# Two attention layers on one core: keys and values as three one-pass fp32r products of split operands

## The chip, the cores and the metric

The kernel runs on one core of a Trainium2 chip. Its engines are TensorE (PE), VectorE (DVE), ScalarE (ACT), GpSimd (POOL) and SyncE (SP, which only issues DMA here). The metric is the device time of one execution in microseconds.

## What is computed

Two layers follow each other. The first (`L0`) mixes x (16 x 64 x 256) with itself, guided by a context `ctx_2048` of the same shape; the second (`L1`) is a transformer block whose keys and values come from the context:

```python
x_q = einsum('oc,bcn->bno', w_qk, y);  x_k = einsum('oc,bcn->bon', w_qk, x)
x_v = einsum('oc,bcn->bon', w_v, x) + b_v
attention = softmax(x_q @ x_k);  attention /= 1e-07 + attention.sum(axis=1)
x_r = x_v @ attention
x   = x + relu(w_t @ (x - x_r) + b_t)                      # layer 0

q = layer_norm(x, ln1) @ q_w + q_b                         # layer 1, 16 heads of 16
k = encoder @ k_w + k_b
v = encoder @ v_w + v_b
hidden = softmax(q k^T / 4, masked) @ v @ cproj_w + cproj_b + x
out = hidden + gelu(layer_norm(hidden, ln2) @ fc_w + fc_b) @ proj_w + proj_b
```

All inputs are fp32 (the mask is boolean). The change touches only how `k` and `v` are formed from the encoder states, which are the context.

## The kernel before, in words

The 16 batches are taken as N = 8 pairs of 128 rows. Every engine walks the same list of steps `t` (`for t in STEPS`, -1 to 20), written out by hand; what an engine does in a step stands in its block in a fixed order, and an instruction that waits holds up all that follow it on that engine.

Steps 0 to 8 hold layer 0. In step t PE makes the energies of pair t (`gx,ys`), the projections of pair t+1 (`rows,gram` and `wtvT,rows`) and the mix of pair t-1 (`att,us`); DVE makes the row maxima (`nmax`, L683), copies the projections out of PSUM (`gx` L688, `uext` L696), takes reciprocals (`rinv` L604) and normalises (`mixn`, `rin`); ACT makes the exponentials (`att`, L443); POOL scales (`us`, L344), adds the residual (L325) and finds the inverse deviation (`rstd`, L308) that DVE's `xn` (L641, x1_norm) waits for; POOL's bias addition (L333) waits in turn for `xn`. From step 9 on (AT = 9) layer 1's attention runs, and from step 15.6 on the MLP.

Keys and values are made in between, in twelve units (`UNITS`, L207) that all pass through one PSUM bank, FILL. For each half of the tokens (h = 0, 1; 512 tokens) there are two "ctx" units, which turn two pairs of context rows each (`ident,ys`, L826) and which ACT copies to `ctxT` (L417); two "keys" units of two 512-column fp32 products each (L833); and two "values" units of four 256-column products each (L840). The next unit waits until ACT has emptied the bank (`free_fill`, L809). The tables at L208 to L211 place them: ctx units of the first half in steps -1 and 0, keys in 0 and 1, values in 1 and 2; ctx units of the second half in steps 4 and 6, keys in 7 and 8, values in 9 and 11. `wk` and `wv` are the fp32 weights of keys and values.

The MLP's weights and inputs are already split: a high part rounded to fp32r and the remainder as a low part (`high_part` on DVE, L636; `low_part` on POOL, L320), multiplied as high-high, high-low and low-high. `SPLIT` (L215) puts one weight part into each of the steps 1 to 7; the buffers `ff[0]`, `ff[1]` are used only once the MLP runs.

Of the kernel before, what the change touches and what calls it, by code (L numbers as in the profile page):

```python
# [13 lines left out]
P = 128  # L14
# [13 lines left out]
def xattn_two_layers(nc, A, out):  # L28
# [24 lines left out]
    with ExitStack() as ctx:  # L53
# [3 lines left out]
        def sem(name):  # L57
# [18 lines left out]
        keys_b = sb("keys_b", [P, G, 2])  # L76
        half_power = sb("half_power", [P, 1])
        wq = sb("wq", [P, G, D])
        wk = sb("wk", [P, G, D])
        wv = sb("wv", [P, G, D])  # L80
        wc = sb("wc", [P, G, D])

        wstage = sb("wstage", [P, 2, W])
# [9 lines left out]

        rows = sb("rows", [P, N, D])
        ys = sb("ys", [P, N, D])
        ctxT = sb("ctxT", [P, G, TOK])
        keys = sb("keys", [P, G, 2, N * P])
        vals = sb("vals", [P, N, 2, HP, 2 * HD])
        gx = sb("gx", [P, 2, D])
# [28 lines left out]
        act_ff = ys[:, 0:4, :].rearrange("p (k a) d -> p k (a d)", k=2)  # L128
        ff = [sb("ff_hi", [P, M, TOK], F32R), sb("ff_lo", [P, M, TOK], F32R)]

        psum = ctx.enter_context(nc.psum_tensor("psum", [P, 8, BANK], F32))

        PROJ0, ENERGY, MIX, WTX, TURN, FILL = 0, 1, 3, 5, 6, 7
# [18 lines left out]
            "mask_ready", "mask_zeroed", "is_row_ready", "select_ready", "parity_ready", "keys_b_ready",  # L152
                                                                   "stored"))
        S = {k: sem(k) for k in (
            "part_hi part_lo ctx_turned ctx_ready keys_made keys_ready values_made values_ready "
            "proj_made proj_ready energy_made energy_max energy_exp rowsum_inv scaled_u mixed wtx_made colsum_ln "
            "colsum_inv mix_normed relu_in relu_out x1_ready x1_stats x1_meanvar x1_vareps x1_rstd x1_normed x1_turned "
            "x1t_ready queries_made queries_ready x1_plus_bias scores_made scores_max scores_shifted "
# [9 lines left out]
        def bank(n):  # L168
            return psum[:, n, :]
# [41 lines left out]
        FILL_C = {N: 9, AT: 10}  # L211

        UNITS_BEFORE = [9, 11]
        WARM_UP = 6
        SPLIT = {1: 0, 2: 1, 3: 2, 4: 3, 5: 4, 6: 5, 7: 6, AT + 5: 7}  # L215

# [67 lines left out]
        def _(pool):  # L284
# [42 lines left out]
            def x1_plus_bias(n):  # L327
# [4 lines left out]
                wait(pool, "x1_normed", n + 1)  # L332
                pool.tensor_tensor(rows[:, n, :], rows[:, n, :], cproj_b[:], ALU.add).then_inc(S["x1_plus_bias"], 1)  # L333

            for t in STEPS:

                n = t
                if 0 <= n < N:

# [7 lines left out]
                if 0 <= t - 2 < N - 1:  # L347
                    residual(t - 2)
                if t == 0:
                    for name, w, s in (("cproj_b", cproj_b, "cb"), ("proj_b", proj_b, "pb")):  # L350
                        src = A["L1_xattn_" + name].rearrange("(o d) -> o d", o=1).broadcast_to([P, D])
                        pool.dma_start(w[:], src).then_inc(w_loaded[s], 16)
# [50 lines left out]
        def _(act):  # L403
# [7 lines left out]
            def fill(unit):  # L411
                kind, h, i = unit
                if kind == "ctx":
                    wait(act, "ctx_turned", 2 * h + i + 1)

                    wait(act, "values_made", 2 * h)
                    act.copy(ctxT[:, :, 2 * i * P:2 * (i + 1) * P].rearrange("p g (a t) -> p a g t", a=2),  # L417
                             bank(FILL).rearrange("p (a g t) -> p a g t", a=2, g=G)).then_inc(S["ctx_ready"], 1)
                if kind == "keys":
                    wait(act, "keys_made", 2 * h + i + 1)  # L420
                    if h == i == 0:
                        act.wait_ge(keys_b_ready, G)
                    for a in range(2):
                        identity(keys[:, i, a, h * TOK:(h + 1) * TOK], bank(FILL), keys_b[:, i, a:a + 1],
                                 parity[:, a:a + 1], "keys_ready")
                if kind == "values":
                    wait(act, "values_made", 2 * h + i + 1)
                    if h == i == 0:
                        act.wait_ge(zeros_ready, 3)
                    n = NH * h + 2 * i  # L430
                    for e in range(2):
                        src = psum[e * C:(e + 1) * C, FILL, :].rearrange("p (a i b d) -> p a i b d", a=2, b=2, d=HD)
                        for b in range(2):
                            act.copy(vals[b * C:(b + 1) * C, n:n + 2, e, :, b * HD:(b + 1) * HD],
                                     src[:, :, :, b, :]).then_inc(S["values_ready"], 1)
# [126 lines left out]
        def _(dve):  # L562
# [64 lines left out]
            def inverse_of_sum(n, i):  # L627
# [2 lines left out]
                dve.reciprocal(pinv[:, n % 2, HEAD_HALVES[i]],  # L630
                               psums[:, n % 2, HEAD_HALVES[i]]).then_inc(S["probs_inv"], 1)

            def high_part(c):
                dve.wait_ge(part_loaded[c % 2], 16 * (c // 2 + 1))
                src, hi, lo = part(c)
                dve.tensor_copy(hi, src).then_inc(S["part_hi"], 1)  # L636
# [38 lines left out]

            for t in STEPS:

                n = t
                if 0 <= n < N:
                    for e in range(2):  # L680
# [5 lines left out]
                if 0 <= n < N:  # L686
                    wait(dve, "proj_made", n + 1)
                    dve.tensor_copy(gx[:, n % 2, :], halfbank(PROJ0, 0)).then_inc(S["proj_ready"], 1)  # L688
                    wait(dve, "scaled_u", 4 * (n - 1))
                    if n == 0:  # L690
                        dve.wait_ge(wtbv_made, 1)
                        dve.tensor_copy(wtbv[:], psum[:, SETUP_WTBV, 0:P]).then_inc(wtbv_ready, 1)
                        dve.wait_ge(wtbv_ready, 1)
                        dve.wait_ge(zeros_ready, 3)
                    dst = uext[:, n % 2, :, :].rearrange("p j (b c) -> p j b c", b=3)[:, :, 0:3:2, :]
                    dve.tensor_tensor(dst, halfbank(PROJ0, 1).rearrange("p (j b c) -> p j b c", j=2, b=2),  # L696
                                      wtbv[:].rearrange("p (b c) -> p b c", b=2).unsqueeze(1)
                                      .broadcast_to([P, 2, 2, C]), ALU.add).then_inc(S["proj_ready"], 1)
                if 0 <= t - 4 < N - 3:
                    x1_norm(t - 4)  # L700
                if 0 <= t < N:
# [9 lines left out]
                if t == 0:  # L711
# [5 lines left out]
                    for g in range(G):  # L717
                        dve.tensor_scalar(keys_b[:, g, :], parity[:], col(K_B + g), None,
                                          ALU.mult).then_inc(keys_b_ready, 1)
                if 0 <= t < N and t in SPLIT:  # L720
                    high_part(SPLIT[t])
                if t == 5:
# [59 lines left out]
        def _(pe):  # L782
# [26 lines left out]
            def free_fill(i):  # L809

                if i > 0:
                    kind, h, k = UNITS[i - 1]
                    wait(pe, *{"ctx": ("ctx_ready", 2 * h + k + 1), "keys": ("keys_ready", 2 * (2 * h + k + 1)),
                               "values": ("values_ready", 4 * (2 * h + k + 1))}[kind])

            def fill(i):
# [10 lines left out]
                                               ys[:, n, g * P:(g + 1) * P], ident[:])  # L827
                    ins.then_inc(S["ctx_turned"], 1)
                if kind == "keys":
                    pe.wait_ge(w_loaded["k"], 16)  # L830
                    wait(pe, "ctx_ready", 2 * (h + 1))
                    for c in range(G):
                        ins = mm(bank(FILL), wk[:, c, k * P:(k + 1) * P], ctxT[:, c, :], c == 0, c == G - 1)  # L833
                    ins.then_inc(S["keys_made"], 1)
                if kind == "values":
                    pe.wait_ge(w_loaded["v"], 16)
                    for a in range(2):
                        tok = slice((2 * k + a) * P, (2 * k + a + 1) * P)
                        for c in range(G):
                            ins = mm(halfbank(FILL, a), ctxT[:, c, tok], wv[:, c, :], c == 0, c == G - 1)  # L840
                    ins.then_inc(S["values_made"], 1)

            def mlp_unit(h, unit):
# [217 lines left out]
```

## Time and profile before

| | us |
|---|---|
| median of three runs | 170.68 |
| lowest, highest | 170.66, 171.85 |
| the profiled execution | 171.03 |
| its span in the trace | 169.2 |

Busy, of the span: PE 146.0 us (86%), DVE 101.1 (60%), ACT 98.6 (58%), POOL 87.0 (51%). The chain of work that ended last lies on PE for 57%, on POOL for 17% and on DVE for 9%. "Idle before" in a row is the time that the engine waited, with the instruction that released it. An fp32 matmul is recorded as two matmuls, so "x4" in the trace are two products of the program; an fp32r matmul is recorded once. Recorded durations of PE overlap, so costs are read from one start to the next.

### The profile page before, as it was taken

The numbers are of one execution on the slowest core, as the hardware profiler recorded it, in microseconds if no ns is written. First come the engines' busy times: TensorE is split into PE (matmuls) and PEld (weight loads), VectorE is DVE, ScalarE is ACT, GpSimd is POOL, SyncE is SP. The second block draws the span as 40 slices with busy tenths as digits, with TensorE's granted clock in tenths as the row PEclk, the third lists the DMA queues.
The fourth block names the chain that finished last, engine by engine and source line by source line (L and its number), as shares of the span: only waits on it lengthen the run. The fifth ranks groups of instructions, "written<-read, shape, count | busy, mean of one in ns | idle before, by whom it ended". The sixth has DMA issues, their size and how long they took to land.

```text
span 169.2 us, 3520 instructions
## 1 busy us (share of the span) xinstructions
PE 146.0 (86%) x1260; PEld 111.3 (66%) x1260; DVE 101.1 (60%) x243; ACT 98.6 (58%) x242; POOL 87.0 (51%) x146
## 2 busy tenths in 40 slices
PE   7599999999986888197998665957999999999993
PEld 6365678788754264074675544645787999888993
DVE  2435525897975343990589797795678521488221
ACT  2017977789769755735778667966967333344000
POOL 8935617468888952572431976799361634000000
PEclk9969999999999999759999999999999999999999
DMA  1995320202101200000000000000000010000001
GB/s 50 344 326 175 66 62 0 66 0 62 43 25 62 62 0 0 0 6 0 0 4 6 0 4 0 4 0 0 4 0 0 4 61 32 31 0 6 31 31 62
DMA packets 6786, 6.89 MB, mean 41 GB/s; under 512 B 1044, under 2 KB 6194, under 8 KB 6770
## 3 DMA queue, kind: packets, MB, share of 16 engines
q1 hardware_dynamic: 5808, 5.85, 11.1%
q10 hardware_dynamic: 674, 0.56, 1.0%
q0 software_dynamic: 288, 0.27, 0.9%
q8 instruction: 10, 0.16, 0.4%
q14 instruction: 6, 0.05, 0.1%
HBM read 5.62 MB, written 1.05 MB: 39 GB/s over the span
## 4 chain that ended last, share of the span: by engine, by line
PE 57%; POOL 17%; DVE 9%; issue 7%; DMA 4%; ACT 3%; ACTq 1%; POOLq 0%
PE psum L784 53%; DMA ys<-in_ctx_dram 4%; POOL probs L381 4%; POOL us L344 3%; POOL rstd L308 2%; PE psum L1019 2%; POOL wfc_lo L320 2%; POOL wpj_lo L320 1%; DVE smax L738 1%; POOL hidT_lo L372 1%; POOL rows L325 1%; POOL rows L389 1%; DVE psums L625 1%; DVE probs L749 1%; DVE xn L641 1%
## 5 line engine op out<-in xcount | busy, mean ns | idle before, releaser
L381 POOL TENSOR_TENSOR probs<-probs,pinv 128x512 f32<-128x512 f32 x16 | 16.5, 1055 | 9.7 <-DVE pinv L630 9.7
L344 POOL TENSOR_SCALAR us<-uext,rinv 128x128 f32<-128x128 f32 x32 | 12.4, 399 | 13.9 <-DVE rinv L604 13.3
L784 PE MATMUL psum<-wpj_hi,ff_hi 128*128 128x256 f32 x64 | 18.3, 287 | 0.0
L784 PE MATMUL psum<-wpj_hi,ff_lo 128*128 128x256 f32 x64 | 18.1, 283 | 0.0
L784 PE MATMUL psum<-wpj_lo,ff_hi 128*128 128x256 f32 x64 | 18.1, 283 | 0.0
L398 ACT ACTIVATE ys<-psum,vec 128x512 f32<-128x512 f32 x16 | 10.9, 687 | 9.3 <-PE psum L784 9.2
L683 DVE TENSOR_REDUCE nmax<-psum 128x2 f32<-128x512 f32 x16 | 10.3, 685 | 9.9 <-PE psum L784 9.9
L784 PE MATMUL psum<-att,us 128*128 128x256 f32 x64 | 15.2, 381 | 0.7 <-POOL us L344 0.7
L625 DVE TENSOR_REDUCE psums<-probs 128x8 f32<-128x512 f32 x16 | 10.6, 660 | 8.5 <-ACT probs L540 8.3
L443 ACT ACTIVATE att<-psum,nmax 128x256 f32<-128x256 f32 x32 | 14.7, 471 | 0.3 <-DVE nmax L683 0.2
L784 PE MATMUL psum<-hidT_hi,wfc_hi 128*128 128x512 f32 x32 | 13.2, 414 | 1.1 <-POOL hidT_lo L372 1.1
L784 PEld LDWEIGHTS psum<-att,us 128*128 128x128 f32 x64 | 11.9, 190 | 3.1 <-POOL us L344 1.2
L670 DVE TENSOR_TENSOR rows<-psum,rows 128x256 f32<-128x256 f32 x8 | 3.4, 426 | 16.9 <-PE psum L784 16.9
L661 DVE CAST ff_hi<-ys 128x512 fp32r<-128x512 f32 x16 | 7.3, 457 | 8.9 <-ACT ys L398 8.7
L784 PE MATMUL psum<-hidT_hi,wfc_lo 128*128 128x512 f32 x32 | 12.6, 394 | 0.0
L784 PE MATMUL psum<-hidT_lo,wfc_hi 128*128 128x512 f32 x32 | 12.6, 394 | 0.0
L784 PEld LDWEIGHTS psum<-wpj_hi,ff_hi 128*128 128x128 f32 x64 | 12.1, 189 | 0.1
L784 PEld LDWEIGHTS psum<-wpj_lo,ff_hi 128*128 128x128 f32 x64 | 12.1, 188 | 0.1
L784 PEld LDWEIGHTS psum<-wpj_hi,ff_lo 128*128 128x128 f32 x64 | 12.1, 189 | 0.0
L372 POOL TENSOR_TENSOR hidT_lo<-hidf,hidT_hi 128x256 fp32r<-128x256 f32 x8 | 6.2, 778 | 11.0 <-ACT hidT_hi L534 11.0
L663 DVE TENSOR_TENSOR ff_lo<-ys,ff_hi 128x512 fp32r<-128x512 f32 x16 | 11.1, 692 | 0.5
L540 ACT ACTIVATE probs<-probs 128x512 f32<-128x512 f32 x16 | 9.4, 623 | 2.6 <-DVE probs L749 2.6
(115 smaller groups left out, 367.6 us busy)
## 6 DMA issues: line engine op xcount, KB each, us to landing
wstage<-in_L_xattn_fc_w_dram SPq DMA_DIRECT2D x4, 256.0 KB, 5.2
wstage<-in_L_xattn_proj_w_dram SPq DMA_DIRECT2D x4, 256.0 KB, 2.7
out_dram<-rows SPq DMA_DIRECT2D x8, 128.0 KB, 1.7
ys<-in_ctx_dram SPq DMA_DIRECT2D x1, 512.0 KB, 6.3
rows<-in_x_dram SPq DMA_DIRECT2D x1, 512.0 KB, 7.4
ys<-in_ctx_dram ACTq DMA_DIRECT2D x1, 384.0 KB, 7.0
rows<-in_x_dram SPq DMA_DIRECT2D x1, 384.0 KB, 5.8
wk<-in_L_xattn_k_w_dram SPq DMA_DIRECT2D x1, 256.0 KB, 6.7
```

The lines of the kernel that those rows point to most:

```text
L320: pool.tensor_tensor(lo, src, hi.bitcast(F32), ALU.subtract).then_inc(S["part_lo"], 1)
L344: pool.tensor_scalar(us[:, n % 2, e, j, :], uext[:, n % 2, j, e * C:e * C + P], rinv[:, n % 2, e, j:j + 1], 1.0, ALU.mult, ALU.mult).then_ ...
L372: pool.tensor_tensor(hidT[1][:, :, cols], hidf[:], hidT[0][:, :, cols].bitcast(F32), ALU.subtract).then_inc(S["hid_lo"], 1)
L381: pool.tensor_tensor(half, half, pinv[:, n % 2, k].unsqueeze(2).broadcast_to([P, H // 2, C]), ALU.mult).then_inc(S["probs_ready"], 1)
L398: act.activation(act_ff[:, k % 2, :], bank(k % 4), ACT.Gelu_apprx_tanh, bias=col(FC_B + unit[1])).then_inc(S["gelu_ready"], 1)
L443: act.activation(att[:, n % 2, e, j, :], halfbank(ENERGY + e, j), ACT.Exp, bias=nmax[:, n % 2, e, j:j + 1], accum_out=rsum[:, n % 2, e, j: ...
L540: act.activation(half, half, ACT.Exp, scale=SCALE).then_inc(S["probs_exp"], 1)
L625: dve.tensor_reduce(psums[:, n % 2, HEAD_HALVES[i]], half, AX.X, ALU.add).then_inc(S["probs_sum"], 1)
L661: dve.tensor_copy(ff[0][:, m, :], act_ff[:, k % 2, :]).then_inc(S["ff_hi"], 1)
L663: dve.tensor_tensor(ff[1][:, m, :], act_ff[:, k % 2, :], ff[0][:, m, :].bitcast(F32), ALU.subtract).then_inc(S["ff_lo"], 1)
L683: dve.tensor_reduce(nmax[:, n % 2, e, :], bank(ENERGY + e).rearrange("p (j m) -> p j m", j=2), AX.X, ALU.max, negate=True).then_inc(S["ene ...
L784: return pe.matmul(dst, lhsT, rhs, start=start, stop=stop)
```

## The change

Context, `wk` and `wv` are split in a part rounded to fp32r and a remainder. Both parts live in the buffers `ff[0]` (high) and `ff[1]` (low), which are free until the MLP: context in columns 0 and 1, the key weight in 2, the value weight in 3. Therefore they are called ff_hi and ff_lo in the rows of the changed kernel.

- ACT's copy of the turned context now writes the rounded part. DVE makes the remainder, out of the PSUM bank (`ctx_low`), twice in step 0 and once each in steps 4 and 6. PE's next use of the bank, and the keys units, wait for the remainder.
- DVE rounds each weight (`weight_high`), POOL subtracts (`weight_low`), both in step 0.
- A keys unit is six fp32r products of 512 columns instead of two in fp32; a values unit twelve of 256 instead of four.

```diff
+            def weight_low(w, s):
+                wait(pool, f"w{s}_hi", 1)
+                hi, lo = wkr if s == "k" else wvr
+                pool.tensor_tensor(lo, w[:], hi.bitcast(F32), ALU.subtract).then_inc(S[f"w{s}_lo"], 1)
...
+            def ctx_low(h, i):
+                wait(dve, "ctx_ready", 2 * h + i + 1)
+                cols = slice(2 * i * P, 2 * (i + 1) * P)
+                dve.tensor_tensor(ctxT[1][:, :, cols].rearrange("p g (a t) -> p a g t", a=2),
+                                  bank(FILL).rearrange("p (a g t) -> p a g t", a=2, g=G),
+                                  ctxT[0][:, :, cols].bitcast(F32).rearrange("p g (a t) -> p a g t", a=2),
+                                  ALU.subtract).then_inc(S["ctx_lo"], 1)
+
+            def weight_high(w, s):
+                dve.wait_ge(w_loaded[s], 16)
+                dve.tensor_copy((wkr if s == "k" else wvr)[0], w[:]).then_inc(S[f"w{s}_hi"], 1)
...
-                    wait(pe, *{"ctx": ("ctx_ready", 2 * h + k + 1), "keys": ("keys_ready", 2 * (2 * h + k + 1)),
+                    wait(pe, *{"ctx": ("ctx_lo", 2 * h + k + 1), "keys": ("keys_ready", 2 * (2 * h + k + 1)),
...
                 if kind == "keys":
-                    pe.wait_ge(w_loaded["k"], 16)
-                    wait(pe, "ctx_ready", 2 * (h + 1))
+                    wait(pe, "wk_lo", 1)
+                    wait(pe, "ctx_lo", 2 * (h + 1))
                     for c in range(G):
-                        ins = mm(bank(FILL), wk[:, c, k * P:(k + 1) * P], ctxT[:, c, :], c == 0, c == G - 1)
+                        for a, b in ((0, 0), (0, 1), (1, 0)):
+                            ins = mm(bank(FILL), wkr[a][:, c, k * P:(k + 1) * P], ctxT[b][:, c, :],
+                                     c == 0 and a + b == 0, c == G - 1 and a == 1)
                     ins.then_inc(S["keys_made"], 1)
                 if kind == "values":
-                    pe.wait_ge(w_loaded["v"], 16)
+                    wait(pe, "wv_lo", 1)
```

On DVE, steps -1 and 0 read as follows before; the row of maxima (`nmax`) opens step 0, and a name in brackets is what an instruction waits for:

```order
L696 TENSOR_TENSOR uext<-psum,wtbv 128x2x2x64 [waits zeros_ready,wtbv_ready]
L683 TENSOR_REDUCE nmax<-psum 128x2 [waits energy_made] x2
L688 COPY gx<-psum 128x256 [waits proj_made]
L696 TENSOR_TENSOR uext<-psum,wtbv 128x2x2x64
L604 RECIPROCAL rinv<-rsum 128x2 [waits energy_exp] x2
L714 COPY vec<-psum 128x22 [waits vec_turned]
```

and now (`ff_lo<-psum,ff_hi` is the context's remainder, `ff_hi<-wk` and `ff_hi<-wv` the rounded weights):

```order
L723 TENSOR_TENSOR uext<-psum,wtbv 128x2x2x64 [waits zeros_ready,wtbv_ready]
L648 TENSOR_TENSOR ff_lo<-psum,ff_hi 128x2x2x128 [waits ctx_ready]
L655 CAST ff_hi<-wk 128x512 [waits w_loaded_k]
L710 TENSOR_REDUCE nmax<-psum 128x2 [waits energy_made] x2
L715 COPY gx<-psum 128x256 [waits proj_made]
L723 TENSOR_TENSOR uext<-psum,wtbv 128x2x2x64
L648 TENSOR_TENSOR ff_lo<-psum,ff_hi 128x2x2x128 [waits ctx_ready]
L655 CAST ff_hi<-wv 128x512 [waits w_loaded_v]
L616 RECIPROCAL rinv<-rsum 128x2 [waits energy_exp] x2
L744 COPY vec<-psum 128x22 [waits vec_turned]
```

One remainder and one cast stand ahead of the maxima, one of each between `uext` and the reciprocals that POOL waits for.

At the end of step 4 and the start of step 5, DVE before:

```order
L595 BN_AGGR mv<-stats 128x2 [waits x1_stats]
L636 CAST wfc_hi<-wstage 128x512 [waits part_loaded1]
L683 TENSOR_REDUCE nmax<-psum 128x2 [waits energy_exp,energy_made] x2
L688 COPY gx<-psum 128x256 [waits proj_made]
L696 TENSOR_TENSOR uext<-psum,wtbv 128x2x2x64 [waits scaled_u]
L641 TENSOR_SCALAR xn<-rows,mv,rstd 128x256 [waits x1_rstd]
```

and now:

```order
L607 BN_AGGR mv<-stats 128x2 [waits x1_stats]
L648 TENSOR_TENSOR ff_lo<-psum,ff_hi 128x2x2x128 [waits ctx_ready]
L660 CAST wfc_hi<-wstage 128x512 [waits part_loaded1]
L710 TENSOR_REDUCE nmax<-psum 128x2 [waits energy_exp,energy_made] x2
L715 COPY gx<-psum 128x256 [waits proj_made]
L723 TENSOR_TENSOR uext<-psum,wtbv 128x2x2x64 [waits scaled_u]
L665 TENSOR_SCALAR xn<-rows,mv,rstd 128x256 [waits x1_rstd]
```

The remainder, which waits for ACT's copy of the turned context, came in ahead of the cast, the maxima and `xn`. In step 6 it stands in the same way between `mv` and the cast, ahead of the maxima of step 7.

On PE the values unit of step 9 had four products, and has now twelve, of which the last six stand here (`ff_hi` alone is high times high):

```order
L816 MATMUL psum<-ff_hi 128x256
L816 MATMUL psum<-ff_lo,ff_hi 128x256
L816 MATMUL psum<-ff_hi,ff_lo 128x256
L816 MATMUL psum<-ff_hi 128x256
L816 MATMUL psum<-ff_lo,ff_hi 128x256
L816 MATMUL psum<-ff_hi,ff_lo 128x256
L916 MATMUL psum<-ident,xn 128x128 x2
```

against, before:

```order
L784 MATMUL psum<-wv,ctxT 128x256 x4
L880 MATMUL psum<-ident,xn 128x128 x2
```

Each fp32 product has become three; the turn of x1 (`ident,xn`) still stands behind the unit.

## Rows read from the trace of the kernel before

**Rows 1.** Busy time by stretch: stretch, then busy us (count) of PE, PEld, DVE, ACT, POOL; clock, DMA.

```profile
30.00:40.00 10.00, 10.00 (x60) 7.92 (x58) 9.23 (x26) 7.92 (x27) 6.18 (x13) 1.00 0.09 28
...
50.00:60.00 10.00, 7.22 (x23) 3.56 (x22) 5.17 (x17) 8.81 (x24) 8.45 (x17) 1.00 0.18 52
```

**Rows 2.** PE in order of time, MLP: start, duration, operation, [idle before].

```profile
116.46 0.40 PE L784 MATMUL psum<-hidT_lo,wfc_hi 128*128 128x512 f32 x1
...
118.79 0.40 PE L784 MATMUL psum<-hidT_hi,wfc_lo 128*128 128x512 f32 x1
...
132.20 0.28 PE L784 MATMUL psum<-wpj_hi,ff_lo 128*128 128x256 f32 x1
...
133.63 0.28 PE L784 MATMUL psum<-wpj_hi,ff_lo 128*128 128x256 f32 x1
```

**Rows 3.** PE in order of time, steps 0 to 2: keys, values and the mixes behind them.

```profile
13.68 1.98 PE L784 MATMUL psum<-ctxT,wk 128*128 128x512 f32 x4
...
17.64 1.94 PE L784 MATMUL psum<-ctxT,wk 128*128 128x512 f32 x4
19.42 1.89 PE L784 MATMUL psum<-att,us 128*128 128x256 f32 x8
...
25.53 1.89 PE L784 MATMUL psum<-wv,ctxT 128*128 128x256 f32 x8
27.26 1.89 PE L784 MATMUL psum<-att,us 128*128 128x256 f32 x8
```

**Rows 4.** All engines in order of time, steps 0 and 1: DVE and ACT.

```profile
12.14 1.29 DVE L683 TENSOR_REDUCE nmax<-psum 128x2 f32<-128x512 f32 x2 [2.37 <-PE psum L784]
...
12.74 0.59 ACT L417 COPY ctxT<-psum 128x512 f32<-128x512 f32 x1 [1.75 <-PE psum L826]
...
13.96 0.41 DVE L696 TENSOR_TENSOR uext<-psum,wtbv 128x256 f32<-128x256 f32 x1
...
19.62 1.45 ACT L409 ACTIVATE keys<-psum,keys_b,parity 128x512 f32<-128x512 f32 x2 [0.21 <-PE psum L784]
```

**Rows 5.** Groups by line and shape, DVE and POOL: busy us, mean ns of one.

```profile
L749 DVE TENSOR_TENSOR probs<-psum,smax 128x512 f32<-128x512 f32 x16 | 10.3, 684 | 0.2
...
L636 DVE CAST wfc_hi<-wstage 128x512 fp32r<-128x512 f32 x4 | 1.7, 417 | 0.0
...
L320 POOL TENSOR_TENSOR wfc_lo<-wstage,wfc_hi 128x512 fp32r<-128x512 f32 x4 | 5.1, 1272 | 0.0
```

**Rows 6.** All engines in order of time, end of step 4 and step 5.

```profile
39.46 0.58 ACT L417 COPY ctxT<-psum 128x512 f32<-128x512 f32 x1
39.51 1.29 DVE L683 TENSOR_REDUCE nmax<-psum 128x2 f32<-128x512 f32 x2 [0.27 <-PE psum L784]
...
42.17 0.41 DVE L641 TENSOR_SCALAR xn<-rows,mv,rstd 128x256 f32<-128x256 f32 x1 [0.71 <-POOL rstd L308]
...
42.67 0.73 POOL L333 TENSOR_TENSOR rows<-rows,cproj_b 128x256 f32<-128x256 f32 x1 [0.53 <-DVE xn L641]
```

**Rows 7.** All engines in order of time, steps 6 and 7.

```profile
51.18 0.58 ACT L417 COPY ctxT<-psum 128x512 f32<-128x512 f32 x1
...
52.92 0.46 ACT L443 ACTIVATE att<-psum,nmax 128x256 f32<-128x256 f32 x1
...
57.09 1.96 PE L784 MATMUL psum<-x1T,wq 128*128 128x512 f32 x4 [0.62 <-issue]
```

**Rows 8.** All engines in order of time, the seam of the two layers.

```profile
71.98 0.40 PE L784 MATMUL psum<-maskrow,select 32*128 32x256 bf16 x4 [3.69 <-DVE probs L749]
...
73.89 3.22 PE L784 MATMUL psum<-wv,ctxT 128*128 128x256 f32 x8
...
78.22 1.98 PE L784 MATMUL psum<-x1T,wq 128*128 128x512 f32 x4 [0.90 <-ACT x1T L409]
...
88.93 1.23 DVE L738 TENSOR_REDUCE smax<-psum 128x16 f32<-128x1024 f32 x1 [0.52 <-PE psum L784]
```

**Rows 9.** Busy time by stretch, PE alone: stretch, PE busy us (count), granted clock, DMA.

```profile
74.00:75.00 1.00, 1.00 (x4) 0.50 0.00 0
```

More of the change, by code:

```diff
@@ L78, in xattn_two_layers @@
         wq = sb("wq", [P, G, D])
-        wk = sb("wk", [P, G, D])
-        wv = sb("wv", [P, G, D])
         wc = sb("wc", [P, G, D])
@@ L95, in xattn_two_layers @@
         ys = sb("ys", [P, N, D])
-        ctxT = sb("ctxT", [P, G, TOK])
         keys = sb("keys", [P, G, 2, N * P])
@@ L129, in xattn_two_layers @@
         ff = [sb("ff_hi", [P, M, TOK], F32R), sb("ff_lo", [P, M, TOK], F32R)]
+        ctxT = [ff[0][:, 0:G, :], ff[1][:, 0:G, :]]
+        wkr = [ff[k][:, 2:3, :].rearrange("p o (g n) -> p (o g) n", g=G) for k in range(2)]
+        wvr = [ff[k][:, 3:4, :].rearrange("p o (g n) -> p (o g) n", g=G) for k in range(2)]
+        wk = sb("wk", [P, G, D])
+        wv = sb("wv", [P, G, D])
         psum = ctx.enter_context(nc.psum_tensor("psum", [P, 8, BANK], F32))
@@ L154, in xattn_two_layers @@
         S = {k: sem(k) for k in (
-            "part_hi part_lo ctx_turned ctx_ready keys_made keys_ready values_made values_ready "
+            "part_hi part_lo wk_hi wk_lo wv_hi wv_lo ctx_turned ctx_ready ctx_lo keys_made keys_ready values_made values_ready "
             "proj_made proj_ready energy_made energy_max energy_exp rowsum_inv scaled_u mixed wtx_made colsum_ln "
@@ L213, in xattn_two_layers @@
         UNITS_BEFORE = [9, 11]
+        CTX_LOW = (4, 6)
         WARM_UP = 6
@@ L333, in x1_plus_bias @@
                 pool.tensor_tensor(rows[:, n, :], rows[:, n, :], cproj_b[:], ALU.add).then_inc(S["x1_plus_bias"], 1)
+            def weight_low(w, s):
+                wait(pool, f"w{s}_hi", 1)
+                hi, lo = wkr if s == "k" else wvr
+                pool.tensor_tensor(lo, w[:], hi.bitcast(F32), ALU.subtract).then_inc(S[f"w{s}_lo"], 1)
             for t in STEPS:
+                if t == 0:
+                    weight_low(wk, "k")
                 n = t
@@ L349, in _ @@
                 if t == 0:
+                    weight_low(wv, "v")
                     for name, w, s in (("cproj_b", cproj_b, "cb"), ("proj_b", proj_b, "pb")):
@@ L416, in fill @@
                     wait(act, "values_made", 2 * h)
-                    act.copy(ctxT[:, :, 2 * i * P:2 * (i + 1) * P].rearrange("p g (a t) -> p a g t", a=2),
+                    act.copy(ctxT[0][:, :, 2 * i * P:2 * (i + 1) * P].rearrange("p g (a t) -> p a g t", a=2),
                              bank(FILL).rearrange("p (a g t) -> p a g t", a=2, g=G)).then_inc(S["ctx_ready"], 1)
@@ L676, in _ @@
             for t in STEPS:
+                if t == 0:
+                    ctx_low(0, 0)
+                    weight_high(wk, "k")
                 n = t
@@ L698, in _ @@
                                       .broadcast_to([P, 2, 2, C]), ALU.add).then_inc(S["proj_ready"], 1)
+                if t == 0:
+                    ctx_low(0, 1)
+                    weight_high(wv, "v")
                 if 0 <= t - 4 < N - 3:
@@ L719, in _ @@
                                           ALU.mult).then_inc(keys_b_ready, 1)
+                if t in CTX_LOW:
+                    ctx_low(1, CTX_LOW.index(t))
                 if 0 <= t < N and t in SPLIT:
@@ L839, in fill @@
                         for c in range(G):
-                            ins = mm(halfbank(FILL, a), ctxT[:, c, tok], wv[:, c, :], c == 0, c == G - 1)
+                            for x, y in ((0, 0), (0, 1), (1, 0)):
+                                ins = mm(halfbank(FILL, a), ctxT[x][:, c, tok], wvr[y][:, c, :],
+                                         c == 0 and x + y == 0, c == G - 1 and x == 1)
                     ins.then_inc(S["values_made"], 1)
```

## The prediction

> **What bounds the kernel now.** I read the busy time by stretch first, then the instructions in order of time. Over 30 to 40 us DVE is busy 9.23 of 10 us and PE's records cover all 10 [rows 1]: two engines are full in the stretch where the change adds work to one and takes it from the other. So a sum of PE time saved says nothing yet; each place has to be asked which wait ends last there. There are four: step 0 of the first layer (12 to 30 us), the turn of context rows in steps 4 and 6 (38 to 57 us), and the seam between the layers with its values units (72 to 89 us). From 116 us on, the MLP has no changed instruction.
>
> **What one unit saves on PE.** A values unit is four fp32 products of 256 columns, eight records, 25.53 to 27.26: 1.73 us, 0.216 a record [rows 3]. A keys unit is two fp32 products of 512 columns, four records of twice that, 1.73 us again; from 17.64 to the next work at 19.42 the trace has 1.78 [rows 3], so 0.05 is a gap that stays. What the new units cost is shown by the MLP, which already multiplies split fp32r operands three ways: at 512 columns 10 starts lie in 118.79 - 116.46 = 2.33 us, 0.233 each; at 256 columns 12 starts in 133.63 - 132.20 = 1.43 us, 0.119 each [rows 2]. Six of the first are 1.40 us, twelve of the second 1.43 us. A keys unit saves 0.33 us, a values unit 0.30 us; all eight save 2.5 us. At 256 columns, three fp32r passes cost nearly as much as the fp32 they replace, so the prize is small from the start.
>
> The Trainium skill ("TensorE: Matmul & The Clock Gate", section "Back-to-back issue gap") gives N / 2.4 + 2.5 ns for a matmul on its own at the full clock, 216 and 109 ns at these sizes. By it the units would take 1.30 and 1.31 us, and my total would be about 0.5 us lower; the rows of this kernel's own fp32r products are 0.233 and 0.119, and I go by them.
>
> **Step 0: PE waits for DVE.** Before, the first keys unit starts at 13.68, soon after ACT's second copy of the turned context, which ends at 12.74 + 0.59 [rows 3, 4]. Now it needs both low parts and the weight's low part. The price of a low part on DVE is taken from the nearest row, a subtraction out of PSUM at 128x512: 0.684 us; a cast of that size to fp32r takes 0.417 on DVE, a subtraction to fp32r 1.272 on POOL [rows 5]. The first low part and the first weight cast, 1.1 us together, fall into DVE's idle 2.37 us before 12.14 [rows 4] and cost nothing; were that cover gone, 1.1 us. The weight's low part then runs on POOL to about 13.5, before anyone asks for it. The second low part is queued behind two maxima, gx and uext: 13.96 + 0.41 + 0.68 = 15.05, so the keys unit starts at 15.1, **1.4 us late**, and ends 1.4 - 0.33 = 1.07 late. The next energies and their exponentials on ACT are that late. The second keys unit gives back 0.33, but the values unit behind it waits for its bank, which ACT empties from 19.62 on, after step 1's exponentials [rows 4]: that copy is 1.07 late too. Less two values units, 0.60, this leaves +0.47 at the mix at 27.26. Behind the second low part on DVE stand also a second weight cast and the reciprocals that POOL's scaling waits for; those come 1.2 us later, but the mix that needs them (19.42) is itself later. I take **+0.5**. Bounds: 0 if the low part costs only a cast's 0.42 and the rest sinks into the small idles at 39.5 and 42 us [rows 6], and 1.1 if ACT and DVE keep the whole delay.
>
> **Step 4: DVE waits for ACT.** (Times here and for step 6 are those of before, without the start's +0.5.) The low part is put ahead of DVE's weight cast and of the maxima of step 5 (39.51). It waits for ACT's copy, 39.46 + 0.58 = 40.04 [rows 6]. So: low part 40.07 to 40.75, cast to 41.17, maxima from 41.2, **1.7 us late**. What stands behind them on DVE is gx, uext and then xn, which before waited 0.71 us for POOL's rstd and started at 42.17 [rows 6]; 0.71 of the delay goes into that wait: xn starts at 41.2 + (42.17 - 0.71 - 39.51) = 43.15, 0.98 late. POOL waits for this xn (idle 0.53 before its bias addition at 42.67), and then does its low part of the MLP weight and the next scaling, without a pause. This ring POOL, DVE, POOL sets the pace of steps 4 to 7, so **+1.0** is passed on. Bounds 0.7 (low part at 0.42) and 1.6 (at 1.27, POOL's price for the same operation).
>
> **Step 6: the same again.** ACT's copy ends at 51.18 + 0.58 = 51.76; low part and cast bring the maxima of step 7 to 52.9; the first of the two (half of 1.29) is ready at 53.55. ACT's exponentials, which before began at 52.92 behind ACT's own chain, start at 53.6: **+0.65** on top [rows 7]. From them hang DVE's reciprocal and relu input, ACT's x1T and so the queries product at 57.09, which waits (0.62 idle) [rows 7]. On POOL's ring alone it would be 0.4; the exponentials decide. Bounds 0.4 and 1.2. The keys unit in between (0.33 saved) lies in PE's idle time and gives nothing; nor does the one in step 8, behind which PE idles 3.69 us for DVE before 71.98 [rows 8]. The loads of the MLP weights wait for POOL's low parts and move with them.
>
> **The seam.** The values unit at 73.89 runs at a granted clock of 0.50, the 1.2 GHz level [rows 9], and its eight records take 3.22 us; right behind it come the turn of x1 and ACT's x1T, for which PE waited 0.90 before 78.22 [rows 8]. No row shows fp32r at that level. Sixteen column passes become twelve; between the full-clock 0.30 and a quarter of 3.22, 0.8, I take **-0.45**, since the clock comes back before its end. The last values unit, in step 11, is followed by scores for which DVE waited 0.52 before 88.93 [rows 8]: all of **-0.30** is passed on.
>
> **Sum.** +0.5 + 1.0 + 0.65 - 0.45 - 0.30 = +1.4 us. The profiled execution took 171.03 (span 169.2), 0.35 over the median of 170.68; on the median the forecast is 172.1 us, 0.8% slower.
>
> **Rivals.**
> - *Not slower: the ring has more room than it shows.* If POOL's ring and not DVE sets every step from 4 on, DVE's late maxima cost only what exceeds its waits. Against it: that wait was 0.71 us at 42.17 where 1.7 is asked. From 1.7 us of slack on it would decide; then both middle terms fall and 0.5 - 0.75 remains, 170.4 us. Chance 0.18.
> - *The clock.* PE now idles 1.4 us before the first keys unit. If the granted clock fell there, each unit until it rose would take about 3.2 us for 1.7, as at 73.89 [rows 8, 9]; a keys and a values unit or what stands between them, +2.4 on the rest: 174.5 us. For it: 3.69 us of idleness stand ahead of the half clock there. Against it: 1.4 us is shorter, and between 50 and 60 us PE was idle for 2.8 of 10 us, 0.62 of it before 57.09, at a clock of 1.00 [rows 1, 7]. The skill's same page (section "Part 1: The HAM clock gate") also has idleness lower the clock. Chance 0.05.
> - *Nothing is absorbed.* Steps 4 and 6 cost 1.7 and 2.1 in full, because the exponentials and not xn carry on each time: 0.5 + 3.8 - 0.75 = 3.5, 174.2 us. Chance 0.07.
> - *As summed:* 0.70, by itself 171.2 to 173.0.
>
> **The numbers.** Range 170.3 to 173.4. 1% of the median is 1.7 us, about what a measurement of this kernel tells from no change, so the line to "slower" is at 172.4. A third of my own case lies above it (0.23), and the clock and the full delays (0.12): 0.35. Faster by 1% would need 169.0; even all 2.5 us saved with no delay gives 168.2, and the first rival's lower edge leaves 0.04. The rest, 0.61, is within 1%. It reaches from just below the first rival's 170.4 to 173.4, beyond my own case's upper end; the last two rivals and the first one's lower edge, under 0.2, lie outside.
>
> **What would show it.** After: keys unit from about 15.1 us with DVE named as releaser; low parts of 0.65 to 0.7 us on DVE; an idle time of about 1.1 us on DVE before the third and fourth, ended by ACT; maxima of step 5 near 41.7 and of step 7 near 54.4 (start delay included); x1T products at 59 rather than 57.1. It is wrong if fp32r products between fp32 ones take more than the MLP's spacing, if DVE meets ACT's copy already done, or if POOL's ring swallows the delay.

## The result

The changed kernel takes 172.62 us (median of 20 runs, 170.78 to 174.8) where the kernel before, run beside it on the same chip, takes 171.13 (169.91 to 173.29): ratio 1.0068, 95% interval 1.0034 to 1.0101. That is slower, by less than the 1% that a measurement here tells from no change. The forecast was 172.1 us and a ratio of 1.008. The medians go over all executions and differ by 1.5 us; the ratio, here and for every run below, compares only the executions outside a slower state, which 6 of the 20 of after were in, and stands for 1.2 us (0.6 to 1.7).

The profiled execution of after took 174.69 us, 2.1 more than its median, with a span of 172.9, against 171.03 and 169.2 before. So the difference in span, 3.7 us, must not be read as the change's price; it is taken apart below. The busy times of after, over the whole span:

```profile
PE 147.5 (85%) x1284; PEld 115.5 (67%) x1284; DVE 104.8 (61%) x249; ACT 98.7 (57%) x242; POOL 89.6 (52%) x148
```

**Step 0** (all engines, in order of time: start, duration, engine, line, operation, [idle before and what ended it]), the counterpart of [rows 3, 4]:

```profile
14.91 0.68 DVE L648 TENSOR_TENSOR ff_lo<-psum,ff_hi 128x512 fp32r<-128x512 f32 x1
...
15.74 0.47 PE L816 MATMUL psum<-ff_hi 128*128 128x512 f32 x1 [1.37 <-DVE ff_lo L648]
16.05 0.40 PE L816 MATMUL psum<-ff_lo,ff_hi 128*128 128x512 f32 x1
...
21.00 1.46 ACT L421 ACTIVATE keys<-psum,keys_b,parity 128x512 f32<-128x512 f32 x2
...
28.04 1.89 PE L816 MATMUL psum<-att,us 128*128 128x256 f32 x8
```

PE stands still for 1.37 us and the row names DVE's low part as what ended it. ACT's copy of the keys from the second keys unit (21.00) has no wait in brackets any more; before, it had one of 0.21 [rows 4].

**Steps 4 and 5**, the counterpart of [rows 6], same view:

```profile
40.23 0.58 ACT L429 CAST ff_hi<-psum 128x512 fp32r<-128x512 f32 x1
...
40.84 0.69 DVE L648 TENSOR_TENSOR ff_lo<-psum,ff_hi 128x512 fp32r<-128x512 f32 x1 [1.20 <-ACT ff_hi L429]
41.21 0.73 POOL L330 TENSOR_TENSOR rows<-rows,rout 128x256 f32<-128x256 f32 x1
41.45 0.77 DVE L660 CAST wfc_hi<-wstage 128x512 fp32r<-128x512 f32 x1
42.14 1.27 DVE L710 TENSOR_REDUCE nmax<-psum 128x2 f32<-128x512 f32 x2
...
44.00 0.40 DVE L665 TENSOR_SCALAR xn<-rows,mv,rstd 128x256 f32<-128x256 f32 x1
...
44.48 0.73 POOL L338 TENSOR_TENSOR rows<-rows,cproj_b 128x256 f32<-128x256 f32 x1 [1.57 <-DVE xn L665]
```

DVE, which was full here, now waits 1.20 us for ACT; `xn` no longer waits for POOL's `rstd`, and POOL waits 1.57 us for `xn` where it waited 0.53 [rows 6].

**Steps 6 and 7**, the counterpart of [rows 7]:

```profile
53.61 0.69 DVE L648 TENSOR_TENSOR ff_lo<-psum,ff_hi 128x512 fp32r<-128x512 f32 x1 [1.20 <-ACT ff_hi L429]
...
54.22 0.67 DVE L660 CAST wpj_hi<-wstage 128x512 fp32r<-128x512 f32 x1
...
54.81 1.28 DVE L710 TENSOR_REDUCE nmax<-psum 128x2 f32<-128x512 f32 x2
...
55.52 0.47 ACT L455 ACTIVATE att<-psum,nmax 128x256 f32<-128x256 f32 x1 [0.69 <-DVE nmax L710]
...
59.50 1.96 PE L816 MATMUL psum<-x1T,wq 128*128 128x512 f32 x4 [1.22 <-issue]
```

ACT's exponentials did not wait before [rows 7]; now the row names DVE's maxima, 0.69 us.

**The seam**, the counterpart of [rows 8]:

```profile
74.40 0.40 PE L816 MATMUL psum<-maskrow,select 32*128 32x256 bf16 x4 [3.68 <-DVE probs L781]
...
76.16 0.56 PE L816 MATMUL psum<-ff_hi 128*128 128x256 f32 x1
...
78.86 0.63 PE L916 MATMUL psum<-ident,xn 128*128 128x128 f32 x2
80.39 3.77 PE L816 MATMUL psum<-x1T,wq 128*128 128x512 f32 x4 [0.90 <-ACT x1T L421]
```

Busy time of after by stretch, PE alone (stretch, PE busy us (count), granted clock, DMA share, GB/s):

```profile
82.00:84.00 2.00, 2.00 (x4) 0.50 0.00 0
84.00:86.00 2.00, 2.00 (x12) 1.00 0.00 0
```

The queries product that took 1.98 us before [rows 8] takes 3.77 here: the clock is still 0.50 up to 84 us, where before it was 1.00 again by 78.

**Where 3.7 us went.** Marks found in every trace cut the span into stretches: DVE's first maxima (before at 12.14, [rows 4]), those of step 3 (30.24), the first row maximum `smax` of the second layer (68.27), its fourth (88.93, [rows 8]) and the start of the last result row (166.66). In after the first maxima start at 12.77, the last row at 170.31, and between them:

```profile
31.02 1.29 DVE L710 TENSOR_REDUCE nmax<-psum 128x2 f32<-128x512 f32 x2 [1.94 <-PE psum L816]
...
70.69 1.19 DVE L770 TENSOR_REDUCE smax<-psum 128x16 f32<-128x1024 f32 x1
...
92.58 1.23 DVE L770 TENSOR_REDUCE smax<-psum 128x16 f32<-128x1024 f32 x1 [0.21 <-PE psum L816]
```

The first maxima start 0.63 us later. The part in front of them differs from trace to trace by more (they start between 11.27 and 13.17 in the traces below), and the first low part did not delay them: they start 1.85 us behind the first energies of the step, before (10.29) as after (10.92). The stretches, in us:

| stretch | before | after | difference | forecast |
|---|---|---|---|---|
| 1: first maxima to those of step 3 | 18.10 | 18.25 | +0.15 | +0.5 |
| 2: to first `smax` of layer 2 | 38.03 | 39.67 | +1.64 | +1.65 |
| 3: to fourth `smax` | 20.66 | 21.89 | +1.23 | -0.75 |
| 4: to the last result row | 77.73 | 77.73 | 0.00 | 0 |

With the start's 0.63 these are the 3.65 us between the two last rows. Stretch 3 holds the clock's late return: 3.77 - 1.98 = 1.79 for the queries product alone. In two of the experiments that have the same fp32r products and an early return it is 20.01 and 19.82 (runs 1 and 2), -0.65 and -0.84 against before. With these the change's own part is 0.15 + 1.64 - 0.75 = about +1.0 us. But the same two traces are 0.35 and 0.50 us longer in stretch 4, where the clock falls once more (see runs 5 and 6), so that stretches 3 and 4 together give only -0.30 and -0.34; counted so, the change costs about +1.5. Whether this lengthening of stretch 4 belongs to the change is not shown. The measured 1.2 us (0.6 to 1.7) fits both.

### The profile page after: what moved, and what is told of

Its sections match the earlier page's. It is cut to its first block, busy times and chain, and to the rows that moved or that the text cites. A ratio compares the mean times of both kernels' runs of the same rounds, so it can differ in the third digit from the quotient of the medians.

```text
span 172.9 us, 3576 instructions
## 1 busy us (share of the span) xinstructions
PE 147.5 (85%) x1284; PEld 115.5 (67%) x1284; DVE 104.8 (61%) x249; ACT 98.7 (57%) x242; POOL 89.6 (52%) x148
## 3 DMA queue, kind: packets, MB, share of 16 engines
HBM read 5.62 MB, written 1.05 MB: 39 GB/s over the span
## 4 chain that ended last, share of the span: by engine, by line
PE 57%; POOL 14%; DVE 12%; issue 8%; ACT 4%; DMA 3%; POOLq 0%; DVEq 0%; ACTq 0%
PE psum L816 53%; POOL probs L393 4%; DMA vec_rows<-in_L_xattn_b_t_dram 3%; POOL us L355 2%; POOL rstd L313 2%; PE psum L1055 2%; POOL wfc_lo L325 1%; DVE smax L770 1%; POOL hidT_lo L384 1%; ACT x1T L421 1%; DVE mixn L622 1%; POOL rows L401 1%; DVE psums L637 1%; DVE nmax L710 1%; DVE probs L781 1%
## 5 line engine op out<-in xcount | busy, mean ns | idle before, releaser
L816 PE MATMUL psum<-x1T,wq 128*128 128x512 f32 x16 | 9.6, 728 | 2.8 <-issue 1.9
```

The lines of the kernel that those rows point to most:

```text
L816: return pe.matmul(dst, lhsT, rhs, start=start, stop=stop)
```

## The experiments

Each run was timed beside the kernel before (median 171.63 us for runs 1 to 4, 171.01 for 5 to 8). "After" is always the changed kernel; stretches are those of the table above, and a table at the end has them for all runs.

### 1. The remainders of steps 4 and 6 one place later

Theory: the two delays come from where the low part stands on DVE, ahead of the maxima, not from its 0.69 us of work. Rival: POOL's ring would have absorbed them anyway.

```
-                if t in CTX_LOW:
-                    ctx_low(1, CTX_LOW.index(t))
...
+                if t - 1 in CTX_LOW:
+                    ctx_low(1, CTX_LOW.index(t - 1))
                 if 0 <= t - 4 < N - 3:
                     x1_norm(t - 4)
```

> The changed kernel with one thing moved: the third and fourth context remainders on DVE stand in steps 5 and 7, behind gx and uext and ahead of xn, where DVE waited 0.71 and 1.74 us for POOL before the change. My theory: steps 4 and 6 cost 1.06 and 0.59 us in the trace of the changed kernel only because DVE stood waiting for ACT's copy with the maxima behind it. Then DVE's two idle times of 1.20 us ended by ACT are gone, xn of step 5 and 7 come when POOL's rstd lets them, and the time falls by 1.65 us, from a ratio of 1.007 to about 0.997 of the kernel before. Rival: the ring through POOL sets the pace and DVE's late maxima cost nothing. Then the ratio stays at 1.007.

Measured: 171.21 us, ratio 0.9989 (0.995 to 1.0028). Stretch 2 is 37.97 us, before 38.03, after 39.67: the whole +1.64 is gone. DVE of this run, in order of time:

```profile
38.23 0.45 DVE L660 CAST wfc_hi<-wstage 128x512 fp32r<-128x512 f32 x1
...
40.81 0.68 DVE L648 TENSOR_TENSOR ff_lo<-psum,ff_hi 128x512 fp32r<-128x512 f32 x1
41.59 0.41 DVE L665 TENSOR_SCALAR xn<-rows,mv,rstd 128x256 f32<-128x256 f32 x1
...
51.43 0.68 DVE L648 TENSOR_TENSOR ff_lo<-psum,ff_hi 128x512 fp32r<-128x512 f32 x1
...
53.23 0.41 DVE L665 TENSOR_SCALAR xn<-rows,mv,rstd 128x256 f32<-128x256 f32 x1 [1.12 <-POOL rstd L313]
```

The same two operations of 0.68 us now meet ACT's copy already done, and lie in the time in which `xn` waits for POOL's `rstd` anyway: at 53.23 it still waits 1.12 us behind the second. The work is the same; the place cost 1.64 us. This speaks against the ring's slack: with the remainders ahead of the maxima nothing of these 1.64 us was swallowed. Moving them had one more effect: the casts behind them, 0.77 and 0.67 us in after, are back at 0.45 and 0.39 here, so a part of the delay was theirs (last section). The whole time came 0.2% above the 0.997 expected, within its interval.

### 2. The second remainder of step 0 ahead of gx and uext

Theory: PE's wait in step 0 is DVE's order, and shrinks by the 0.8 us of `gx` and `uext`. The weight cast for the values moves behind `keys_b`.

```
+                if t == 0:
+                    ctx_low(0, 1)
                 n = t + 1
...
-                if t == 0:
-                    ctx_low(0, 1)
-                    weight_high(wv, "v")
...
+                    weight_high(wv, "v")
```

> The changed kernel with step 0 alone rearranged on DVE: the second context remainder right behind step 0's maxima, the value weight's cast at the end of the step. The first keys unit should start about 0.5 us later than before the change instead of 1.4. My theory, which put the start term at +0.5 (the trace of the changed kernel has only +0.15 by step 3): PE bounds steps 0 to 2, so the 0.9 us come through to step 3 and the ratio falls from 1.007 to about 1.002. Rival: the full DVE and ACT of steps 2 to 4 swallow them, and the ratio stays at 1.007.

Measured: 172.17 us, ratio 1.0055 (1.0017 to 1.0093). DVE and PE of this run in order of time:

```profile
14.62 0.69 DVE L648 TENSOR_TENSOR ff_lo<-psum,ff_hi 128x512 fp32r<-128x512 f32 x1 [0.17 <-ACT ff_hi L429]
...
15.46 0.47 PE L816 MATMUL psum<-ff_hi 128*128 128x512 f32 x1 [0.45 <-DVE ff_lo L648]
```

PE waits 0.45 us instead of 1.37, 0.92 less. Stretch 1 is 17.57 us, 0.68 below after and 0.53 below before; the other 0.24 went into a later turn of the context rows: ACT's copy of it starts 0.84 us behind the first maxima here (14.01), 0.59 in after (13.36). The whole time, expected at 1.002, does not separate this kernel from after (1.0068). Stretch 2 is 39.67, exactly after's: the two parts do not touch each other.

### 3. Both placements

The edits of 1 and 2 together.

> Both rearrangements at once. If the terms add up as I think: -1.65 and -0.9 against the changed kernel, a ratio of about 0.992, faster than the kernel before, since only the savings on PE are left. If either rival holds (POOL's ring, or DVE and ACT full in steps 2 to 4), 0.997 to 1.007.

Measured: 170.1 us, ratio 0.9934 (0.9897 to 0.997). Stretch 1 is 17.57, stretch 2 38.02: the sum of the two, with nothing lost. So the one-pass products do save time once the low parts stand where DVE or ACT is not asked for anything: 0.53 us in stretch 1, and 0.66% in all, which by itself is also under the 1% that a measurement tells from no change, though its interval leaves 1 out.

### 4. fp32 products on the new waits

After, but the keys and values units multiply the unrounded weights by the rounded context in fp32, two and four products as before; the remainders are made and waited for but not used, so the product with the context's remainder is left out of what is computed. The keys unit is shown; the values unit is changed in the same way.

```
-                        for a, b in ((0, 0), (0, 1), (1, 0)):
-                            ins = mm(bank(FILL), wkr[a][:, c, k * P:(k + 1) * P], ctxT[b][:, c, :],
-                                     c == 0 and a + b == 0, c == G - 1 and a == 1)
+                        ins = mm(bank(FILL), wk[:, c, k * P:(k + 1) * P], ctxT[0][:, c, :].bitcast(F32),
+                                 c == 0, c == G - 1)
```

> The changed kernel with all of its splitting and all of its waits, but with PE's keys and values units as two and four fp32 products again, of the fp32 weights with the rounded context; the remainders are made and not used. It measures what the cheaper products on PE give back. My theory: 0.33 and 0.30 us for each of the four units in steps 0 to 2 (1.3 in all, of which the ACT copy of keys may hide a part), 0.5 and 0.3 in the seam, nothing for the two keys units of steps 7 and 8: +1.8 us, a ratio of about 1.017. If PE's units were off the path, the ratio would stay at 1.007.

Measured: 175.1 us, ratio 1.0209 (1.0149 to 1.0268). PE in order of time:

```profile
15.97 1.95 PE L816 MATMUL psum<-ff_hi,wk 128*128 128x512 f32 x4 [1.37 <-DVE ff_lo L648]
...
29.46 1.89 PE L816 MATMUL psum<-att,us 128*128 128x256 f32 x8
```

The wait is again 1.37 us. Stretch 1 is 19.71: with the waits alone it is 19.71 - 18.10 = 1.61 us over before, and after is 19.71 - 18.25 = 1.46 below it. Neither is pure: the keys unit starts 15.97 - 12.74 = 3.23 us behind the first maxima here and 15.74 - 12.77 = 2.97 in after, at the same wait. This 0.26 is again the later turn of the context rows (ACT's copy at 13.59, 0.85 behind the maxima). Without it the delay costs 1.35 and the cheaper units give back 1.20, near the 1.26 that four of them save by the forecast's prices. Stretch 2 is 39.68, as in after: the cheaper keys units of steps 7 and 8 give nothing. The ratio is a little above the 1.017 expected.

### 5 and 6. The clock kept up across the seam

To see the seam without the half clock, eight products nobody reads are put into PE's 3.7 us of idleness, once into the kernel before and once into after:

```
                 if t == N:
                     turn_x1(N - 3)
+                    wait(pe, "relu_in", N)
+                    for _ in range(8):
+                        mm(halfbank(WTX, 0), ident[:], wq[:, 0, :])
```

> The kernel before with one addition: eight fp32 products of 256 columns on PE, into a free PSUM bank and read by nobody, in the stretch where PE idles 3.69 us for DVE between the two layers. They do no work of the kernel and should take 3.4 us of that idle time. Theory: the granted clock of 0.50 in the seam comes from this idle time, and the time at which it returns (76.3 us in the trace of before, about 83 in that of the changed kernel) is chance and not the change's doing. Then the clock stays at 1.00, scores, turns and the values unit behind it take about half, and the ratio to the kernel before is about 0.988. Rival: other waits (ACT, DVE) set the seam and PE's clock there is hidden: 1.000, or slower if the idle time is overrun.

> The changed kernel with the same eight idle products. If the clock's return is chance, its ratio falls from 1.007 by about as much as the kernel before gains, or a little more, to 0.993, and the difference of the two kernels without the clock's part is left: the terms of steps 0, 4 and 6 (+0.15, +1.06, +0.6 us) less 0.3 us for each of two values units at full clock, +1.2 us or 0.7% over the kernel before with the same addition. If the change itself lengthens the half-clock stretch, the two come closer together than that.

Measured: on the kernel before 169.45 us, ratio 0.9924 (0.9892 to 0.9956); on after 170.84, ratio 0.9985 (0.9954 to 1.0016). PE of the kernel before with these products:

```profile
68.03 3.62 PE L784 MATMUL psum<-wq,ident 128*128 128x256 f32 x16
71.87 0.29 PE L784 MATMUL psum<-maskrow,select 32*128 32x256 bf16 x4 [0.23 <-DVE probs L749]
```

Its busy time by stretch, PE alone:

```profile
74.00:76.00 2.00, 1.10 (x7) 1.00 0.01 4
...
94.00:96.00 2.00, 2.00 (x7) 0.50 0.00 0
```

The clock is 1.00 through the seam, and stretch 3 is 18.55 us for the kernel before and 17.96 for after: the one-pass products are worth 0.59 us in it, the forecast's 0.30 twice. But both kernels gained less in all than the expectations had it (0.988 and 0.993). In both profiles the clock falls to 0.50 once more near 94 us (last row), in stretch 4, which is 77.71 us for before (as without the products) and 78.00 for after (+0.27). Such a second fall is in every trace but that of the kernel before: from about 93 to 102 us in runs 1, 2, 4, 5 and 6, after 103 us in after and runs 3, 7 and 8, and once more near 107 in run 1. Where it comes late, stretch 4 is 77.72 to 77.82 us; where it comes early, 78.00 to 78.23 in the changed kernels and 77.71 in run 5. And the profiled execution of before gained 2.1 us in the seam, its median 171.01 - 169.45 = 1.56. How often each pattern of the clock occurs over many executions no profile tells; this remainder stays open.

Between these two kernels the ratio is 0.9985 / 0.9924 = 1.006, about 1.0 us, where each of the two ratios is known to about 0.5 us. By stretches the change costs 0.17 + 1.66 - 0.59 + 0.29 = 1.5, or 1.2 without the stretch that has no changed instruction. The 1.006 with the clock held across the seam is close to the 1.0068 without: these runs give no sign that the change makes the half clock at the seam longer.

### 7. Only the remainder of step 6 left in its place

> The changed kernel with only the third remainder moved from step 4 to step 5, behind gx and uext; the fourth stays in step 6. Read in the trace, from the maxima of step 3 to the first score maximum: 38.03 us before the change, 39.67 after it. Theory, by the offsets of the changed kernel's rows: step 4 makes 1.06 and step 6 0.6 of these 1.64, so 38.6 here. If step 6 alone could cost everything once step 4 is free (the slack of the ring being used only once), 39.2 or more; if step 6 costs nothing alone, 38.0.

```
-                if t in CTX_LOW:
-                    ctx_low(1, CTX_LOW.index(t))
+                if t == 6:
+                    ctx_low(1, 1)
...
+                if t == 5:
+                    ctx_low(1, 0)
```

Measured: 172.57 us, ratio 1.011 (1.0041 to 1.0178), from two executions; the whole time does not separate it from after. Its two marks do:

```profile
30.28 1.29 DVE L710 TENSOR_REDUCE nmax<-psum 128x2 f32<-128x512 f32 x2 [1.94 <-PE psum L818]
...
68.86 1.19 DVE L772 TENSOR_REDUCE smax<-psum 128x16 f32<-128x1024 f32 x1
```

Stretch 2 is 68.86 - 30.28 = 38.58 us: step 6 alone costs +0.55 over the kernel before, and step 4 the other 1.09.

### 8. Both placements and the clock held

> Both rearrangements of the remainders on DVE (third and fourth in the waits of steps 5 and 7, the second behind step 0's maxima) and the eight idle products. If the gains add up: 0.993 from the rearrangements, less 1.2% from the clock, about 0.981 of the kernel before. If the clock's gain is lost elsewhere, 0.99.

Measured: 167.84 us, ratio 0.9836 (0.9788 to 0.9883), the fastest of all, below both kernels; against the kernel before with the same eight products it is 0.9836 / 0.9924 = 0.991. Its clock falls too, later than in runs 5 and 6 (PE alone, by stretch; stretch 4 is 77.82 us):

```profile
104.00:106.00 2.00, 2.00 (x8) 0.50 0.00 0
```

| kernel | us | ratio (95%) | 1 | 2 | 3 | 4 | half clock at the seam |
|---|---|---|---|---|---|---|---|
| before | 171.13 | 1 | 18.10 | 38.03 | 20.66 | 77.73 | 6.8 |
| after | 172.62 | 1.0068 (1.0034-1.0101) | 18.25 | 39.67 | 21.89 | 77.73 | 10.2 |
| 1: steps 4, 6 later | 171.21 | 0.9989 (0.995-1.0028) | 18.24 | 37.97 | 20.01 | 78.08 | 6.8 |
| 2: step 0 earlier | 172.17 | 1.0055 (1.0017-1.0093) | 17.57 | 39.67 | 19.82 | 78.23 | 6.8 |
| 3: both | 170.1 | 0.9934 (0.9897-0.997) | 17.57 | 38.02 | 21.78 | 77.72 | 10.2 |
| 4: fp32 products | 175.1 | 1.0209 (1.0149-1.0268) | 19.71 | 39.68 | 21.17 | 78.22 | 6.8 |
| 5: before, clock held | 169.45 | 0.9924 (0.9892-0.9956) | 18.10 | 37.96 | 18.55 | 77.71 | 0 |
| 6: after, clock held | 170.84 | 0.9985 (0.9954-1.0016) | 18.27 | 39.62 | 17.96 | 78.00 | 0 |
| 7: step 4 later | 172.57 | 1.011 (1.0041-1.0178) | 18.18 | 38.58 | 21.78 | 77.72 | 10.2 |
| 8: both, clock held | 167.84 | 0.9836 (0.9788-0.9883) | 17.34 | 37.96 | 17.96 | 77.82 | 0 |

(Stretches and the last column, the time in us at a granted clock of 0.50 around the seam, worked out from the clock in stretches of 2 us, are those of each kernel's one profiled execution.)

## Why the prediction was right, step by step

**What a unit saves: right.** In after the keys units' products start 0.23 us apart and the values units' 0.119, between fp32 work, as in the MLP [rows 2]. With the clock held the two values units of the seam gave 0.59 us, forecast 0.60. The figures of the Trainium skill ("TensorE: Matmul & The Clock Gate", section "Back-to-back issue gap"), 216 and 109 ns, are below what these units show as they were below the MLP's.

**Step 0: the mechanism right, the size off.** PE's delay came as worked out: +1.43 at the keys unit (15.74 - 13.68 - 0.63 for the later start), forecast 1.4. The low part took 0.68, forecast 0.68. But the mix at 28.04 is only 0.15 late, forecast 0.47. The step that failed is "that copy is 1.07 late too". ACT's instruction in front of the copy did come 1.08 late (20.91 - 19.20 - 0.63):

```profile
19.20 0.21 ACT L443 ACTIVATION_READ_ACCUMULATOR att<-psum,nmax 128x1 f32 x1
...
20.91 0.21 ACT L455 ACTIVATION_READ_ACCUMULATOR att<-psum,nmax 128x1 f32 x1
```

(first row before, second after). But before, the copy stood 0.42 us behind it, waiting for PE (the 0.21 in the brackets of [rows 4]); in after PE's keys unit was done and the copy stands 0.09 behind. So 0.33 of the delay went into this wait, and the copy came 0.75 late (21.00 - 19.62 - 0.63). The bracket stood in [rows 4] and was not used. Run 4 measured the pieces: 1.61 us for the delay and 1.46 given back, 0.26 of both from a later start; together +0.15.

**Step 4: right.** With the 0.78 us taken off by which after ran later already (0.63 + 0.15), the maxima came 42.14 - 39.51 - 0.78 = 1.85 late, forecast 1.7, and `xn` 44.00 - 42.17 - 0.78 = 1.05, forecast 0.98. The low part took 0.69 as priced, but the cast behind it 0.77, not 0.42: that was not foreseen (last section). Run 7, set against after, gives the step 1.09, forecast 1.0.

**Step 6: right.** ACT's exponentials took over as the path, as forecast; `xn`'s own wait was long enough, they were not. The queries product came 0.58 late beyond step 4's delay (59.50 - 57.09 - 0.78 - 1.05), forecast 0.65; run 7 gives 0.55.

**Keys units of steps 7 and 8: right,** nothing (39.67 and 39.68 with and without them).

**The seam: right in what the change does; its clock was missing from the sum.** From the values unit's first product to the turn of x1 behind it after has 78.86 - 76.16 = 2.70 us, all at half clock; before it was 76.94 - 73.89 = 3.05 us, the end of it at full clock:

```profile
76.94 0.38 PE L880 MATMUL psum<-ident,xn 128*128 128x128 f32 x2
```

That is -0.35 where -0.45 was forecast. Where the clock came back early, stretch 3 fell by 0.65 and 0.84 us (runs 1 and 2), forecast -0.75. But the time at half clock is not fixed: 6.8 us in four traces, 10.2 in three (runs 2 and 3 differ in the remainders of steps 4 and 6 alone, runs 1 and 3 in the order of step 0 alone). The longer one costs 1.8 to 2.1 us in stretch 3; behind the shorter one, or none, stretch 4 is 0.3 to 0.5 longer in runs 1, 2, 4 and 6 (not in 5 and 8). The sum held neither.

**The whole.** The forecast's +1.4 lies near the medians' +1.5 and the ratio's +1.2, but not for its reasons alone: step 0 was 0.35 too dear in it, and stretch 4, put at nothing, is 0.3 to 0.5 longer in four traces of changed kernels. That these two are of a size is luck. Without stretch 4 the stretches give +1.0, with it +1.5, and the interval of the ratio, 0.6 to 1.7 us, takes in both. No run measured how often each pattern of the clock occurs in either kernel, so its share of the whole is open.

**The rivals.** *The ring has more room than it shows*: refuted. It would have let the second stretch stand near 38.0; it was 39.67, and went to 37.97 when the low parts were moved (run 1). *The clock falls in step 0*: refuted. PE stood for 1.37 us and the clock stayed at its full level, as PE's stretches of after show:

```profile
14.00:15.00 1.00, 0.37 (x3) 1.00 0.66 230
15.00:16.00 1.00, 0.26 (x1) 1.00 0.15 51
```

*Nothing is absorbed*: refuted; steps 4 and 6 cost 1.64 together, not 3.8.

## What to carry to other kernels

Splitting an operand puts an operation on another engine, and its price is set by its place in that engine's order far more than by its length: the same two 0.69 us subtractions cost 1.64 us ahead of the maxima, partly by where they pushed the casts, and nothing behind them. Put the remainder where its source has been ready for a while and where the next instruction would wait anyway; read the brackets of the rows on both sides, since a wait already there (0.21, 0.71) is what a delay is first paid from. An idle gap ahead of a chain of products can be worth more than the change under study: eight unread products here gave 0.8%, the split 0.7% once placed well, and the two together 1.6%.

## What the runs showed of the hardware

**A cast on DVE beside an addition on POOL.** The weight cast of 128x512 to fp32r takes 0.39 to 0.45 us in the kernel before and in run 1. In after, the two that start while POOL's addition of the residual runs take 0.77 and 0.67. Their ends, 42.22 and 54.89, both lie 0.28 us behind the end of that addition (41.21 + 0.73 = 41.94; in step 6 53.88 + 0.73 = 54.61, from this row):

```profile
53.88 0.73 POOL L330 TENSOR_TENSOR rows<-rows,rout 128x256 f32<-128x256 f32 x1
```

In run 7 the cast of step 4 starts before the addition (40.52) and that of step 6 under it (52.05):

```profile
38.83 0.45 DVE L660 CAST wfc_hi<-wstage 128x512 fp32r<-128x512 f32 x1
...
52.41 0.66 DVE L660 CAST wpj_hi<-wstage 128x512 fp32r<-128x512 f32 x1
```

All traces agree: the casts of steps 4 and 6 take 0.66 to 0.78 us in after and runs 2, 4, 6 and 7 (step 6) where they start under the addition, and 0.39 to 0.45 where they do not. The Trainium skill ("SBUF — State Buffer", the section on its two separate sides) says that DVE and GpSimd share a pair of ports that, for the instructions that use it, one of them holds alone while the other waits. That agrees with these rows; which ports this cast uses no run here shows.

**Half clock and one-pass products.** At a granted clock of 0.50 the 256-column fp32r products of the seam start about 0.21 us apart, 1.8 times the 0.119 of the full clock; the last of after's unit:

```profile
78.65 0.41 PE L816 MATMUL psum<-ff_hi,ff_lo 128*128 128x256 f32 x1
```

**The clock after idleness.** 3.69 and 3.68 us without a matmul ahead of the mask products ended in a clock of 0.50 each time, 1.37 us in step 0 did not lower it; with eight products in the gap it stayed at 1.00 there, and then fell later in all three such traces, near 94 us in runs 5 and 6 and near 104 in run 8. The length of the gap alone does not decide it. The same gap of 1.72 us stands in the kernel before, where the clock stayed at 1.00, and in run 5, where it was at 0.50 from about 93.6 us on, with PE at work since 92.04:

```profile
94.26 0.65 PE L784 MATMUL psum<-prT,vals 128*32 128x64 f32 x32 [1.72 <-DVE rows L648]
...
92.04 0.65 PE L784 MATMUL psum<-prT,vals 128*32 128x64 f32 x32 [1.72 <-DVE rows L648]
```

(first row before, second run 5). How long the clock stays at half at the seam, 6.8 or 10.2 us, differs between kernels whose work around it is the same (runs 2 and 3). What decides that was not found.
